# Five stages of an audio tower: averages ahead of weights, a moved router, dense weights loaded in the heads' last trip, quantised chunks normalised ahead

## What is computed

```python
h = ewma_both_ways(x) @ W.T + b                       # a: token means, one-head attention
u = layernorm(h); h = h + attention(u @ Wq.T, u @ Wk.T, u @ Wv.T, rope, causal + 1)
u = layernorm(h)                                      # b: 16 causal heads, and the router
hd = u + rmsnorm(heads(u, 16, causal) @ wo)
top_w, top_i = top_k(softmax(u @ router_w), 2)
dense = hd + rmsnorm((silu(hd @ w1) * (hd @ w3)) @ w2)          # c: dense FFN
moe = rmsnorm(sum_k top_w[k] * expert[top_i[k]](u))             # c: 8 experts
h = h + dense + moe
h = h + local_heads(layernorm(h), window=128) @ Wout  # d: 16 local heads
h = h + qlinear(gelu(qlinear(layernorm(h), w1, b1)), w2, b2)    # e: integers of 127 steps
```

## Time and profile before

| | us |
|---|---|
| median of 3 runs | 1845.01 (1844.80 to 1847.09) |
| the profiled execution | 1847.77 |
| its span | 1846.0 |

### The profile page before, as it was taken

One profiled execution on the slowest core, in us unless ns is written; L12 is line 12 of the kernel. 1 busy time (PEld: TensorE's weight loads), 2 busy tenths in 40 slices (PEclk: granted clock), 3 DMA queues, 4 the chain that ended last, 5 costly groups with the idle time before them and its releaser, 6 DMA issues. The chain is left out here.

```text
span 1846.0 us, 31979 instructions
## 1 busy us (share of the span) xinstructions
PE 1471.7 (80%) x10886; PEld 1161.7 (63%) x10886; DVE 1132.5 (61%) x2505; ACT 700.3 (38%) x1428; POOL 288.7 (16%) x224
## 2 busy tenths in 40 slices
PE   2578777988888978888398999788588978889565
PEld 1467676665555645555287888677476767677435
DVE  3676663775775676673455443566576766758486
ACT  1122231353444434445253553343223423234275
POOL 1111021203003003200000002751212220200000
PEclk9699797898988978989698999889798989899888
DMA  4000015216026117210542333320556252330001
GB/s 125 1 1 1 0 45 135 58 57 174 8 81 164 29 35 199 61 35 2 176 150 63 104 101 104 92 65 7 144 135 167 64 148 52 105 97 2 4 1 67
DMA packets 102314, 141.09 MB, mean 76 GB/s; under 512 B 30307, under 2 KB 91084, under 8 KB 102156
## 3 DMA queue, kind: packets, MB, share of 16 engines
q1 hardware_dynamic: 86034, 120.93, 22.8%
q0 software_dynamic: 12672, 13.45, 2.7%
q10 hardware_dynamic: 3456, 4.77, 0.9%
HBM read 77.17 MB, written 61.27 MB: 75 GB/s over the span
## 5 line engine op out<-in xcount | busy, mean ns | idle before, releaser
L1251 ACT ACTIVATE b_probs<-b_ps 125x500 f32<-125x500 f32 (+1 forms) x352 | 187.2, 568 | 153.7 <-PE b_ps L1114 137.5
L1501 DVE TENSOR_REDUCE b_neg<-b_ps 125x1 f32<-125x500 f32 (+3 forms) x304 | 183.6, 644 | 70.7 <-PE b_ps L1079 61.3
L1073 PE MATMUL b_ps<-b_k_st,b_q_st 96*125 96x500 bf16 (+3 forms) x512 | 153.2, 346 | 40.2 <-DVE b_neg L1501 16.3
L1251 ACT ACTIVATE d_probs<-d_ps 125x504 f32<-125x504 f32 (+1 forms) x176 | 100.4, 589 | 171.7 <-PE d_ps L1114 154.0
L1110 PE MATMUL b_ps<-b_q_st,b_k_st 99*125 99x500 bf16 (+3 forms) x512 | 147.5, 340 | 12.9 <-ACT b_probs L1251 10.6
L1501 DVE TENSOR_REDUCE d_neg<-d_ps 125x2 f32<-125x504 f32 (+2 forms) x176 | 114.9, 677 | 50.6 <-PE d_ps L1076 44.7
L1073 PEld LDWEIGHTS b_ps<-b_k_st,b_q_st 96*125 96x125 bf16 x512 | 75.2, 152 | 81.9 <-DVE b_neg L1501 29.5
L1073 PE MATMUL d_ps<-d_k_st,d_q_st 96*125 96x252 bf16 (+2 forms) x384 | 100.1, 294 | 24.8 <-DMA d_k_st<-scratch_stacks 15.3
L180 PE MATMUL c_ps<-c_hd,c_dw_hi 128*128 128x500 f32 x192 | 80.1, 417 | 45.5 <-DVE c_ag L2164 25.4
L1110 PE MATMUL d_ps<-d_q_st,d_k_st 99*125 99x252 bf16 (+2 forms) x384 | 94.1, 281 | 23.5 <-ACT d_probs L1251 13.8
L1110 PEld LDWEIGHTS b_ps<-b_q_st,b_k_st 99*125 99x125 bf16 x512 | 69.0, 147 | 56.4 <-ACT b_probs L1251 39.3
(11 more groups left out here) (381 smaller groups left out, 4012.9 us busy)
## 6 DMA issues: line engine op xcount, KB each, us to landing
scratch_stacks<-b_part SPq DMA_DIRECT2D x48, 375.0 KB, 4.6
scratch_stacks<-d_part SPq DMA_DIRECT2D x48, 375.0 KB, 4.6
b_q_st<-scratch_stacks SPq DMA_DIRECT2D x16, 562.5 KB, 5.4
b_k_st<-scratch_stacks SPq DMA_DIRECT2D x16, 562.5 KB, 7.0
d_q_st<-scratch_stacks SPq DMA_DIRECT2D x16, 562.5 KB, 5.1
d_k_st<-scratch_stacks SPq DMA_DIRECT2D x16, 562.5 KB, 6.6
c_xrows<-scratch_slots SPq DMA_DIRECT2D x54, 128.0 KB, 2.1
c_ew_raw<-in_L_ffn_ew_dram SPq DMA_DIRECT2D x24, 256.0 KB, 6.6
```

The lines of the kernel that those rows point to most:

```text
L1073: mm = pe.matmul(out, q_st[0:STACK, hh, i * TT:(i + 1) * TT], k_st[0:STACK, hh, k0:k0 + n], start=True, stop=True)
L1251: act.activation(dst, second_out(x, unit), ACT.Exp).then_inc(c["exp"].sem, 1)
L1501: dve.tensor_reduce(dst, ps[:TT, bank, 0:per * n].rearrange("p (m n) -> p m n", n=n), AX_X, ALU.max, negate=True).then_inc(free_sem(t, p), 1)
```

## The change

Stage a: the loads of the two bias rows and of the constant `half` go from SP's queue to ACT's, behind two new loads of the identities, which are now inputs. Pool's identities and its scaling of Wq are gone; its zeroing moves ahead of `early.prepare`. DVE does the first batch's averages, then waits for the weights, then scales Wq.

Stage b: the router's three steps get new times, behind the first maxima and the turn of group 0 and ahead of `max_in`. `hd` and `hdT` take turns. In the last trip, after group 1's rows are weighed, SP loads all dense weights of stage c to a place of their own; stage c then begins with the rows alone, and its low halves lie over the raw weights.

Stage e: the maximum over the partitions is formed by a transpose on PE, a reduction and a copy on DVE and a second transpose. DVE normalises chunks 0 and 1 inside the first of these, then 2 and 3 ahead of the loop, and c + 4 in it, for c + 2 before. ACT starts with a Gelu of one column. The second bias is prepared ahead of the loop.

```diff
-            for k in range(2):
-                sp.dma_start(bias[:, k], io["L0_tok_b"]...).then_inc(load, 16)
-            sp.dma_start(half[:], io["minus_half"]).then_inc(load, 16)
...
         def _(pe):
-            pe.wait_ge(ready, 4)
+            pe.wait_ge(ready, 32)
...
         def _(act):
+            act.dma_start(ident[:], io["ident"]).then_inc(ready, 16)
+            act.dma_start(identb[:], io["identb"]).then_inc(ready, 16)
+            for k in range(2):
+                act.dma_start(bias[:, k], io["L0_tok_b"]...).then_inc(load, 16)
+            act.dma_start(half[:], io["minus_half"]).then_inc(load, 16)
...
         def _(pool):
-            for k, t in enumerate((ident, identb)):
-                pool.memset(t[:], 0.0).then_inc(ready, 1)
-                pool.wait_ge(ready, 2 * k + 1)
-                pool.affine_select(out=t[:], in_=t[:], compare_op=ALU.not_equal, fill=1.0, base=0, ...)
             own.start(pool, c)
+            pool.memset(zeros[:], 0.0).then_inc(zeroed, 1)
             early.prepare("pool", pool)
-            pool.memset(zeros[:], 0.0).then_inc(zeroed, 1)
-            pool.wait_ge(load_w, W_LOADS)
-            pool.tensor_scalar(w_raw[:, 0], w_raw[:, 0], float(D) ** -0.5, None, ALU.mult).then_inc(set_scale, 1)
...
         def _(dve):
+            dve.wait_ge(set_const, 1)
+            dve.wait_ge(load_x, 16)
+            ema(-1, 1)
+            dve.wait_ge(load_w, W_LOADS)
+            dve.tensor_scalar(w_raw[:, 0], w_raw[:, 0], float(D) ** -0.5, None, ALU.mult).then_inc(set_scale, 1)
             dve.wait_ge(set_wT, 1)
...
         steps_of_batch += over(GROUPS + ROWS_OUT_BY, GROUPS + NORMED_BY,
-                               [(name, (i,)) for name in ("hd", "hdT") for i in range(NT)])
+                               [(name, (i - lag,)) for i in range(NT + 1) for name, lag in (("hd", 0), ("hdT", 1))
+                                if 0 <= i - lag < NT])
...
-        steps_of_batch += over(FRONT_AT + 1.1 - GROUPS, FRONT_AT + 1.2 - GROUPS, [("router", ()), ("route", ())])
-        steps_of_batch += [(FRONT_AT + 1.3 - GROUPS, ("place", ())), (0.3, ("table", ()))]
+        steps_of_batch += [(-0.39, ("router", ())), (-0.385, ("route", ())), (-0.3, ("place", ())), (0.3, ("table", ()))]
...
+            elif kind == "weighed" and args[0] == 1 and not local and isinstance(t, int) and t == B - 1:
+                sp.wait_ge(c["parts_out"].sem, at("parts_out", t, which))
+                sp.wait_ge(c["part2"].sem, at("part2", t, which))
+                sp.wait_ge(c["v"].sem, at("v", t, which))
+                sp.wait_ge(c["sec_mm"].sem, at("sec_mm", t, which, 2 * N_SEC))
+                prefetch(sp)
...
+def load_dense(sp, io, dw_raw, dw_in):
+    for e in range(SL):
+        load_slice(sp, io, e, ...)
...
-            weights(0)
             hd_rows(0)
-            for e in range(1, SL):
-                weights(e)
...
         def _(pool):
-            for k, src in ((U, peak_p), (HID, peak_hid)):
-                pool.wait_ge(s["peaked"], k - U + 1)
-                pool.partition_all_reduce(top[:, k:k + 1], src[:], P, reduce_max).then_inc(s["topped"], 1)
...
+            act.activation(warm[:], inv[:, W1:W1 + 1], ACT.Gelu)
             act.wait_ge(s["scaled"], 1)
-            shift_u(0)
-            shift_u(1)
+            for c in range(4):
+                shift_u(c)
...
+            def peak(k, src):
+                pe.wait_ge(s["peaked"], k - U + 1)
+                pe.transpose(ps[0:1, UPB + 1, 0:P], src[:], ident[:]).then_inc(s["peak_row"], 1)
+                pe.wait_ge(s["top_set"], k - U + 1)
+                pe.transpose(ps[:, UPB + 1, P:P + 1], top_rows[:, k - U], ident[0:1, 0:1]).then_inc(s["topped"], 1)
...
             def scale_of(k):
+                dve.wait_ge(s["peak_row"], k - U + 1)
+                link(dve.tensor_reduce(top_row[:, row], ps[0:1, UPB + 1, 0:P], AX_X, ALU.max))
+                dve.tensor_copy(top_rows[:, k - U], top_row[:, row].to_broadcast([1, P])).then_inc(s["top_set"], 1)
+                if k == U:
+                    normalise(0)
+                    normalise(1)
                 dve.wait_ge(s["topped"], k - U + 1)
...
             for c in range(NCH):
-                if c + 2 < NCH:
-                    normalise(c + 2)
                 if c + 1 < NCH:
                     turned(c + 1)
                 if c + 2 < NCH:
                     integers(c + 2)
+                if c + 4 < NCH:
+                    normalise(c + 4)
                 extremes(c)
```

More of the change, by code:

```diff
@@ L525, in step @@
                     dve.wait_ge(c["unit_mm"].sem, unit_done(t, p))
-                if kind == "ema":
-                    rows = x_sb[:, t + which, :]
-                    dve.tensor_scalar(xs[:], rows, 0.1, None, ALU.mult).then_inc(c["xs"].sem, 1)
-                    dve.wait_ge(c["xs"].sem, at("xs", t, which))
-                    dve.tensor_tensor_scan(fwd[:], decay[:], xs[:], x_sb[:, t + which, 0:1], ALU.mult, ALU.add)\
-                       .then_inc(c["scan"].sem, 1)
-                    dve.tensor_tensor_scan(bwd[:, ::-1], decay[:], xs[:, ::-1], x_sb[:, t + which, T - 1:T], ALU.mult,
-                                           ALU.add).then_inc(c["scan"].sem, 1)
-                    dve.wait_ge(c["scan"].sem, at("scan", t, which))
-                    dve.tensor_tensor(ew[:], fwd[:], bwd[:], ALU.add).then_inc(c["ew"].sem, 1)
+                if kind == "ema" and not (isinstance(t, int) and t == -1):
+                    ema(t, which)
                 elif kind == "tok":
@@ L1721, with load_slice, ffn_semaphores @@
 LIVE = 2 * 8000 + 3 * 4096 + 2 * 1024 + 10 * 32 + 2 * SL * WF * 4 + (1 + 2 * GOT * GT) * D * 4
-def ffn_semaphores(nc, keep, sems):
+def load_slice(sp, io, e, up, down, sem):
+    for k, name in enumerate(("1", "3")):
+        src = io[f"L0_ffn_w{name}"][:, e * E_H:(e + 1) * E_H] if e < SL else io[f"L0_ffn_ew{name}"][e - SL]
+        sp.dma_start(up[:, :, k], src.rearrange("(c p) n -> p c n", p=P)).then_inc(sem, 16)
+    src = io["L0_ffn_w2"][e * E_H:(e + 1) * E_H] if e < SL else io["L0_ffn_ew2"][e - SL]
+    sp.dma_start(down, src.rearrange("(c p) n -> p c n", p=P)).then_inc(sem, 16)
+def load_dense(sp, io, dw_raw, dw_in):
+    for e in range(SL):
+        load_slice(sp, io, e, dw_raw[:, e, 0:W_UP].rearrange("p (c k n) -> p c k n", c=KC, k=2),
+                   dw_raw[:, e, W_UP:WF].rearrange("p (c n) -> p c n", c=KC), dw_in[e])
+def ffn_semaphores(nc, keep, sems, dw_in):
     names = ("const_in made_hi made_lo moe_in up_mm down_mm silu gated g_hi "
@@ L1740, in ffn_program @@
         m = Zone(nc, stack, keep, start, end)
+        dw_lo = m.sb("c_dw_lo", [P, SL, WF], F32R)
         hd = [m.sb(f"c_hd{k}", [P, 2, KC, CN], F32R) for k in range(2)]
@@ L1755, in ffn_program @@
         dw_hi = m.sb("c_dw_hi", [P, SL, WF], F32R)
-        dw_raw = Zone(nc, stack, keep, m.place, end).sb("c_dw_raw", [P, SL, WF], F32)
-        dw_lo = m.sb("c_dw_lo", [P, SL, WF], F32R)
         late = Zone(nc, stack, keep, m.place, start + LIVE)
@@ L2314, in stage_quantised @@
         peak_p = m.sb("e_peak_p", [P, 1], F32)
+        warm = m.sb("e_warm", [P, 1], F32)
+        top_row = m.sb("e_top_row", [1, 2], F32)
+        top_rows = m.sb("e_top_rows", [1, 2, P], F32)
         peak_h = m.sb("e_peak_h", [P, NCH, FC], F32)
@@ L2318, in stage_quantised @@
         ps = m.ps("e_ps", [P, 8, BANK])
-        mv, ext, rstd, scale, inv, top = (q[n] for n in ("mv", "ext", "rstd", "scale", "inv", "top"))
+        mv, ext, rstd, scale, inv = (q[n] for n in ("mv", "ext", "rstd", "scale", "inv"))
         W1, W2, U, HID = range(4)
         UPB, HALF_K = 6, FC // 2
-        names = ("loaded zeroed peaked topped scaled normed u_shift u_int u_turned u_ready biased up_mm gelu hid_peak "
+        names = ("loaded zeroed peaked peak_row top_set topped scaled normed u_shift u_int u_turned u_ready biased up_mm gelu hid_peak "
                  "rows_ok q_shift q_ready down_mm added linked stored").split()
@@ L2397, in _ @@
                         turn(c + 1)
+            peak(HID, peak_hid)
             pe.wait_ge(s["gelu"], NCH * FC)
+            pe.wait_ge(s["scaled"], 2)
             pe.wait_ge(s["rows_ok"], 1)
@@ L2426, in scale_of @@
             def scale_of(k):
+                col, row = slice(k, k + 1), slice(k - U, k - U + 1)
+                dve.wait_ge(s["peak_row"], k - U + 1)
[4 more added lines that the diff above has]
+                    normalise(1)
                 dve.wait_ge(s["topped"], k - U + 1)
-                col = slice(k, k + 1)
-                link(dve.tensor_scalar(scale[:, col], top[:, col], MIN_RANGE, 1.0 / QP, ALU.max, ALU.mult))
+                link(dve.tensor_scalar(scale[:, col], ps[:, UPB + 1, P:P + 1], MIN_RANGE, 1.0 / QP, ALU.max, ALU.mult))
                 link(dve.reciprocal(inv[:, col], scale[:, col]))
```

75 lines of the change are left out of this document (40 added, 35 removed).

## The result

Over 20 runs of each, the changed kernel took 1840.45 us (median) and the kernel before 1846.53; the ratio is 0.9968, 95% interval 0.9955 to 0.9981. So the change gained some 6 us where 20.5 were forecast. The direction was right, the time lies outside the range (1806 to 1836), and the gain is less than a third of the one predicted.

What follows compares the result with a forecast made beforehand. PE led the busy shares, but as a mean over differing stages, so each edit was priced in its stretch: -16.3 + 6.3 + 12.6 - 4.5 - 10 - 8.6 = -20.5 us, from 1845.0 to 1824.5; range 1806 to 1836.

Steps and rivals of the forecast that it cites:

- The trips' term: Three heads trips: router and placing in the new slot cost +4.2 us each, +12.6 in all (0 to +7 each).
- the key wait: Sign in the heads' trip: PE's 5.50 us wait for keys grows to about 10 once the router leaves.
- the router's 3.95 is then on the path: Step for each trip: in PE's busy new slot the router adds 3.95 us, less about 0.75 of idle it fills.
- rival C: Trips: PE waits some 4 us or more for placing, then loses clock, 12.7 us per trip; 1850.0 us; chance 0.06.
- Rival A: Trips: the router hides in its new slot, trips cost 0 and the entry +4; 1809.6 us; chance 0.25.
- rival B: Start: a Pool load of some 7 us moves to the power behind the first h; 1831.5 us; chance 0.12.
- The entry: Way into the heads, once: the router no longer overlaps the wait for keys, +6.3 us (+2 to +9).
- Start: Stage a: first h at 17.3 us instead of 33.55, weights at 9.5 at the latest, -16.3 us (-18 to -14).
- hd and hdT: Heads' trips: interleaving updates and transposed stores saves 1.5 us of ACT's wait per trip, -4.5 us (0 to -7).
- Tail and dense start: End of heads to c's first matmul: stores end earlier, rows load first, -10 us (-11.5 to -9).
- Last stage: Stage e: loop ends 9.7 us earlier, second maximum costs 1.1 more, -8.6 us (-10.5 to -6).
- The four idle times: DVE's remaining idle in the last stage's loop: 0.9, 0.9, 2 and 1 us, given as 5.1, from 14.8.

Runs made afterwards that it cites:

- old_router: The changed kernel with router, route and place at their old times ahead of the first maxima: 1810.19 us, 0.9787 of the kernel before.
- only_router: The kernel before with only the new times of router, route and place: 1.0162 of the kernel before, 30 us slower.
- router_early: The changed kernel with only PE's 36 router matmuls back at their old time; route, place and scatter stay in the new slot: 0.9882 of the kernel before.
- a_only: The kernel before with the changed start (stage a, identities as inputs) alone: 0.9931 of the kernel before, 13 us faster.
- place_late: The changed kernel with place and its scatter moved later, to 0.25 of a group, router as changed: 0.9959 of the kernel before.
- no_reduce: The kernel before with Pool's two last-stage all-reduces replaced by a DVE copy, leaving out the maximum over partitions: 0.9943 of the kernel before.
- e_only: The kernel before with the changed last stage alone: 0.9869 of the kernel before, 24 us faster.

## Why the prediction was wrong

**The trips' term was mis-sized: +4.2 forecast, +8.4, +7.3 and +9.7 measured.** That is 12.8 of the 16 us by which the spans missed. The mechanism (the router is free at its old place ahead of the key wait, and on PE's path in the new one) was right: old_router and only_router show both sides of it, and the key wait grew to 11.19 as the prediction said. What failed is the step "the router's 3.95 is then on the path". I took the duration at full clock from the old place, allowed 1 us more for placing, and put the clock at nothing. In the new slot the granted clock falls at the router in every trip. In trips 1 and 3 it falls inside, so the router takes 5.6 us, and what follows is half as fast until some 7 us later; in trip 2 the router takes 4.1 us and the clock is down for some 3.4 us behind it, and again behind a later wait. The three trips before and after, as wholes:

```profile
450.56:481.74 31.18, 30.30 (x282) 21.52 (x281) 20.05 (x42) 14.86 (x32) 0.00 (x0) 1.00 0.17 39
595.08:629.56 34.48, 31.68 (x280) 22.60 (x281) 20.19 (x43) 14.80 (x32) 0.00 (x0) 0.95 0.15 37
741.64:780.64 39.00, 32.41 (x279) 23.00 (x280) 27.04 (x66) 14.76 (x32) 8.60 (x9) 0.91 0.22 64
```

```profile
440.20:479.76 39.56, 38.78 (x320) 29.08 (x319) 25.17 (x82) 15.15 (x33) 14.53 (x13) 0.87 0.26 70
590.68:632.46 41.78, 37.34 (x318) 27.13 (x319) 25.02 (x83) 15.27 (x33) 14.53 (x13) 0.92 0.26 68
744.06:792.75 48.69, 41.60 (x317) 30.61 (x318) 32.88 (x105) 15.11 (x33) 22.42 (x21) 0.79 0.27 79
```

What each trip missed of the full clock is its length times one minus the granted clock: 0, 1.7 and 3.5 us before, 5.1, 3.3 and 10.2 after, 13.4 more. With three times 3.95 for the router that is 25.3, for 25.4 measured. This is an estimate, as PE waits in some of that time and waits changed too; it puts the clock at about half of the loss.

The stretch of the kernel before had shown it, in two rows next to those that I used, with the router in 415.1 to 419.1:

```profile
416.00:420.00 4.00, 4.00 (x34) 3.56 (x33) 0.75 (x3) 0.39 (x1) 3.03 (x1) 0.90 1.04 296
420.00:424.00 4.00, 3.24 (x24) 1.52 (x24) 2.27 (x26) 2.08 (x6) 0.00 (x0) 0.67 0.59 163
424.00:428.00 4.00, 0.26 (x2) 0.15 (x2) 2.48 (x13) 0.02 (x1) 0.56 (x2) 0.76 0.85 224
```

The clock goes down at the router's end, while PE is busy 4.00 of 4 in 416 to 420, and is back soon (1.00 in 423 to 426); the key wait begins only at 424.9, and in it the clock falls a second time (0.52 in 426 to 427). I looked at the second fall alone, the low clock of 428 to 436, and so gave the clock to rival C, with a long wait as its condition. At the old place the first fall cost nothing, since the wait came next. In the new one PE-bound work comes next.

**Rival C** had the right place and half of the mechanism. PE did not wait for placing in the changed kernel's first trip, so its condition (a wait of some 4 us) wasn't met, and the clock fell all the same. In router_early it fell behind waits of 1.7 to 2.0, and in the changed kernel's second trip behind one of 0.73, so "at 1 us nothing of it happens" was wrong too. Its price of 4 us was too high: in 428 to 436 PE was busy for 5.6 of the 8 us, so half rate cost at most 2.8 there. Rival A (the router hides) is refuted by the same rows, rival B by the power at 23.16 and by that of a_only.

**Trip 2** stands apart: neither fewer matmuls nor an early router nor a late place shortened it. PE's first second-pass matmul there waits 3.31 us with no releaser in the profile (1.99 before, 3.92 in router_early), at the step where the program's loop over the trips goes round, and the clock falls behind it. place_late had the old wait back:

```profile
612.75 0.42 PE L1116 MATMUL b_ps<-b_q_st,b_k_st 99*125 99x500 bf16 x1 [3.31 <-issue]
```

```profile
609.80 0.42 PE L1116 MATMUL b_ps<-b_q_st,b_k_st 99*125 99x500 bf16 x1 [1.86 <-issue]
```

The wait is 3.3 to 4.4 us in the five kernels whose scatter runs in the new slot and 1.6 to 2.1 in the other eight, so the longer wait goes with the place and its scatter. What it waits for no row names.

**The entry** was +8.3 for +6.3, inside its ends (+2 to +9); against the kernels of the old router whose entry takes 47.4, the move costs 11.5. The kernel before had 50.6 in its profile, and no_reduce 50.5, where the other five with the router at its old place, a_only and e_only with the same code there among them, had 47.4 or 47.5. The router shows why: in those two it began with the clock at 0.50 and took 7.7 us, in the other five it began at 1.00 and took 5.1 to 5.2. So a difference of 3 us between executions went into my rows. In the new slot the entry's router ran at 0.50 and took the 7.7 us of the forecast.

**Start:** -17.3 for -16.3; but the first h came at 18.0 for 17.3, 15.6 earlier than before, so 1.8 of the 17.3 lie behind it, where the code is the same and the executions of one code differ by up to 3 us. The weights came 2.5 later than I had them, at 12.0; why was not taken apart. **hd and hdT:** -5.8 for -4.5. **Tail and dense start:** -8.2 for -10, outside its ends: from the first new row the stores ended after 13.3 us, where I had 12.2, the rows' load followed by 3.0 for 2.3, and landed in 5.7 for 5.4. **Last stage:** -10.9 for -8.6, outside its ends (-10.5 to -6); DVE's idle time fell to 2.9 and not to 5.1, the second scale was near its price. The four idle times that I listed add up to 4.8 and not to 5.1, and no row gave them. Other executions of the old last stage took longer than the one in my rows: from the first peak to the end 105.9 us in only_router and 107.2 in a_only, for 102.8; the changed stage took 91.9 to 92.3 in every trace. So the gain there is 10.9 to 15, by which execution of the old stage it is taken from.

**c and d** took 4.9 longer in the changed kernel's profile, from c's first copy to the first peak: 831.7 us for 826.8. Kernels with the code of before in that stretch had 825.8, 826.8, 827.7, 828.2 and 831.7, and those with the changed code 827.3 to 831.7, so this looks like the difference from one execution to the next, and not the change.

By the parts, then: the edits other than the router's move are worth some 39 us (old_router), and the move gives back 33 of them. old_router beats both kernels.

## What to carry to other kernels

A step right ahead of a longer wait for a DMA was free here: the wait grew from 5.50 to 11.19 us when the step went, and what the step did to the clock had been free too. Before moving such a step, look at what would stand behind it in the new place. Take the granted clock of the stretch in which a step runs today, and of the one after it, together with its duration: the clock that it leaves behind is part of its price. Price each edit by its own stretch and test it alone, for a sum of gains can hide one large loss.

## What was not expected of the hardware

A wait at the start of the program came from an instruction at its end. With Pool's all-reduce in the last stage the first affine select waited 9.87 us (9.33 in only_router) with no releaser; without it 0.51, at the same code (e_only, no_reduce), though an all-reduce in stage d was left in all of them. The Trainium skill's page "GPSIMD Engine Reference" (section 2.1 Instruction dispatch) tells of an unseen load of about 6 us at the first call of freshly loaded code; the 5.97 ahead of the last stage's all-reduce is of that size, the 9.4 at the start is not, and no row names either. For the change this means that two of its edits took away the same wait: the 13 us of a_only and the 24 of e_only don't add up, since 9.4 us of them are one.

The granted clock fell from 1.00 to 0.50 inside a run of 36 matmuls of 8 columns, with PE busy without a gap. It did so in four of the nine trips with the router in its new slot (changed, only_router, place_late), where the router then took 5.2 to 5.7 us; in the other five the same run ended after 4.1 us at 1.00, and the clock fell at a wait of 0.7 us right behind it. A duration read from one trip does not show this.
